# A fused two-layer transformer kernel: the start of the kernel and of its first phase rearranged

## The reference

```python
x = norm(x + L0_attn_ref(x, ...))          # 16 heads of 8, distance bias, head mask; then two norms and a ReLU FFN
x = norm(x + L0_xattn_ref(x, ctx, ctx, ...))   # windowed attention over ctx
x = norm(x + L0_ffn_ref(x, ...))           # 8 experts, top 2
x = norm(x + L1_attn_ref(x, ...))          # rotary, causal
x = norm(x + L1_xattn_ref(x, ctx, ctx, ...))   # gated recurrence
x = norm(x + L1_ffn_ref(x, ...))           # 8 experts, switch (top 1)
```

## Time and profile before

| | us |
|---|---|
| median of 3 runs (1364.31 to 1366.75) | 1365.14 |
| profiled execution | 1372.58 |
| its span, first to last instruction | 1370.8 |
| PE busy | 1208.5 |
| DVE busy | 1042.2 |
| ACT busy | 863.7 |
| POOL busy | 555.5 |

### The profile page before, as it was taken

The page is one execution under the profiler, slowest core; times in us unless marked ns, Lnnn a source line. Parts: engine busy times, 40 slices in busy tenths (PEclk is TensorE's granted clock), DMA queues, the critical chain, the costliest instruction groups (busy, mean ns, idle before and its releaser), DMA issues. The chain is left out here.

```text
span 1370.8 us, 32006 instructions
## 1 busy us (share of the span) xinstructions
PE 1208.5 (88%) x10253; PEld 826.9 (60%) x10253; DVE 1042.2 (76%) x3184; ACT 863.7 (63%) x2474; POOL 555.5 (41%) x831
## 2 busy tenths in 40 slices
PE   3889999999999999988399987999999979998996
PEld 2456666666666666654266654555555556777996
DVE  3477888788888888875678867999999975665465
ACT  2678887878787878764256634666666654453464
POOL 1232334435353534442400027555565312556287
PEclk9999999999999999988599999999999999999999
DMA  6100000001010000000122222013100000000673
GB/s 267 51 17 11 15 17 19 29 17 32 11 32 16 28 17 17 15 13 13 52 74 80 80 70 95 23 37 93 27 24 21 1 3 1 17 17 27 169 209 97
DMA packets 71490, 63.54 MB, mean 46 GB/s; under 512 B 10510, under 2 KB 61586, under 8 KB 70688
## 3 DMA queue, kind: packets, MB, share of 16 engines
q1 hardware_dynamic: 62768, 45.27, 11.3%
q0 software_dynamic: 6400, 12.63, 3.0%
q10 hardware_dynamic: 2160, 3.60, 0.8%
HBM read 43.00 MB, written 18.98 MB: 45 GB/s over the span
## 5 line engine op out<-in xcount | busy, mean ns | idle before, releaser
L767 PE MATMUL e_bank_turned<-c_matrices,e_probs 128*128 128x128 f32 x1024 | 165.9, 286 | 16.3 <-ACT e_probs_t L999 9.0
L693 POOL TENSOR_TENSOR e_rstd<-e_var_eps,c_minus_half 128x1 f32<-128x1 f32 x128 | 71.2, 572 | 253.6 <-DVE e_var_eps L1040 252.9
L999 ACT ACTIVATE e_probs_t<-e_bank_turned 128x512 f32<-128x512 f32 x256 | 155.1, 606 | 16.0 <-PE e_bank_turned L767 14.6
L1127 DVE TENSOR_REDUCE e_neg_max<-e_bank_scores 128x4 f32<-128x512 f32 x160 | 109.6, 685 | 50.8 <-PE e_bank_scores L810 50.4
L767 PEld LDWEIGHTS e_bank_turned<-c_matrices,e_probs 128*128 128x128 f32 x1024 | 116.6, 145 | 40.0 <-issue 16.1
L777 PE MATMUL e_bank_mix<-e_probs_t,e_values 128*32 128x128 f32 x2048 | 113.2, 294 | 15.6 <-ACT e_probs_t L999 14.8
L958 ACT ACTIVATE e_probs<-e_scores,e_neg_max 128x128 f32<-128x128 f32 x384 | 123.3, 410 | 1.1 <-DVE e_neg_max L1163 1.1
L1771 ACT ACTIVATE d_probs_t<-d_bank_turned 128x512 f32<-128x512 f32 x128 | 77.2, 603 | 66.0 <-PE d_bank_turned L1648 66.0
L953 ACT ACTIVATE e_probs<-e_scores 128x512 f32<-128x512 f32 x128 | 82.1, 642 | 42.0 <-DVE e_scores L1160 40.2
L696 POOL TENSOR_TENSOR e_k_by_place<-e_q_k_k,c_matrices 128x512 f32<-128x512 f32 x64 | 66.7, 1042 | 102.8 <-DVE e_q_k_k L1171 102.8
L1753 ACT ACTIVATE d_probs<-d_scores 128x512 f32<-128x512 f32 x128 | 81.0, 632 | 40.6 <-DVE d_scores L1794 38.9
(11 more groups left out here) (330 smaller groups left out, 3289.2 us busy)
## 6 DMA issues: line engine op xcount, KB each, us to landing
streamed<-in_s_up SPq DMA_DIRECT2D x36, 258.0 KB
m_rows<-scratch_sorted SPq DMA_DIRECT2D x72, 64.0 KB
scratch_expert_out<-m_y SPq DMA_DIRECT2D x72, 64.0 KB
sorted_rows<-scratch_sorted SPq DMA_DIRECT2D x40, 65.0 KB, 2.4
e_x_in<-in_x SPq DMA_DIRECT2D x32, 64.0 KB, 1.9
e_ctx_in<-in_ctx SPq DMA_DIRECT2D x32, 64.0 KB, 2.1
up<-in_m_wgv SPq DMA_DIRECT2D x1, 2048.0 KB
up_b<-in_m_bgv SPq DMA_DIRECT2D x1, 2048.0 KB
```

Source lines behind the costliest of these rows:

```text
L767: last = nc.tensor.transpose(turned_bank[:, j * P:(j + 1) * P], pr[k % 3][:, j, :], c["ident"][:])
L999: nc.scalar.activation(pt[k % 2][:], turned_bank[:], ACT.Copy).then_inc(probs_t_ready, 1)
L1127: nc.vector.tensor_reduce(nmax[k % 4][:], bank, AX.X, ALU.max, negate=True).then_inc(max_ready, 1)
```

## The change

Four things are done at once.

- The head mask is loaded as one row into one partition (8 KB), first of all loads. In the encoder PE spreads it over the partitions of the four banks of `quad` with four matmuls against a row of ones. DVE makes `bias0` out of `quad` at tick -5 of the encoder, and PE's `bank_free` waits for that (`bias_made`) for the first units.
- x and ctx of batches 0 to 3 are loaded from the constants phase, x on SP and ctx on ACT, behind the constants. Their buffers and the `x_loaded` semaphores belong to the constants now.
- The `va` tiles are cleared and their columns set by POOL, ahead of its ticks.
- PE no longer waits for `buffers_set`; ACT waits for it ahead of its first copy into `va`.

```diff
@@ load_constants
-    loads.append((c["bias0"][:], d["head_mask"].partition_broadcast(P)))
+    c["head_mask"], c["ones_row"] = sb("head_mask", [1, HEADS, P]), sb("ones_row", [1, P])
+    loads.insert(0, (c["head_mask"][:], d["head_mask"].rearrange("(o h) t -> o h t", o=1)))
+    c["x_in"], c["ctx_in"] = ring(nc, ctx, "c_x_in", [P, P], 4), ring(nc, ctx, "c_ctx_in", [P, P], 4)
+    c["x_loaded"] = [nc.alloc_semaphore(f"x_loaded{k}") for k in range(4)]
...
             for tile, src in loads[0::2]:
                 sp.dma_start(tile, src).then_inc(loaded, 16)
+            for n in range(4):
+                sp.dma_start(c["x_in"][n][:], dram_tile(d["x"], n)).then_inc(c["x_loaded"][n], 16)
...
             for tile, src in loads[1::2]:
                 act.dma_start(tile, src).then_inc(loaded, 16)
+            for n in range(4):
+                act.dma_start(c["ctx_in"][n][:], dram_tile(d["ctx"], n)).then_inc(c["x_loaded"][n], 16)
...
+            nc.vector.memset(c["ones_row"][:], 1.0)
...
-            nc.vector.scalar_tensor_tensor(out=c["bias0"][:], in0=repeat(c["dist"][:], HEADS), scalar=c["nds"][:],
-                                           in1=c["bias0"][:], op0=ALU.mult, op1=ALU.add).then_inc(made, 1)
-            dve.wait_ge(made, 1)
@@ phase_encode, SP
-            for n in range(4):
-                load(n)
@@ phase_encode, POOL, ahead of the ticks
+            for k in range(3):
+                nc.gpsimd.memset(va[0][k][:], 0.0)
+                last = nc.gpsimd.memset(va[1][k][:], 0.0)
+            last.then_inc(buffers_set, 1)
+            pool.wait_ge(buffers_set, 1)
+            for k in range(3):
+                nc.gpsimd.memset(va[0][k][:, :, DH:DH + 1], 1.0)
+                last = nc.gpsimd.memset(va[1][k][:, :, DH:DH + 1], 1.0)
+            last.then_inc(buffers_set, 1)
@@ phase_encode, PE
                 elif k >= 0:
                     pe.wait_ge(probs_ready, k + 1)
+                else:
+                    pe.wait_ge(bias_made, 1)
...
+            for g in range(G):
+                last = nc.tensor.matmul(quad[:, g, :], lhsT=c["ones_row"][:],
+                                        rhs=c["head_mask"][:, G * g:G * g + G, :].rearrange("o h t -> o (h t)"), start=True, stop=True)
+            last.then_inc(mask_spread, 1)
             pe.wait_ge(act_read, 1)
...
-            pe.wait_ge(buffers_set, 2)
@@ phase_encode, ACT
-            act.wait_ge(buffers_set, 2)
...
                     if (n := at(tick, -7)) is not None:
+                        if n == 0:
+                            act.wait_ge(buffers_set, 2)
@@ phase_encode, DVE
-            for k in range(3):
-                nc.vector.memset(va[0][k][:], 0.0)
-                last = nc.vector.memset(va[1][k][:], 0.0)
-            last.then_inc(buffers_set, 1)
...
-            dve.wait_ge(buffers_set, 1)
-            for k in range(3):
-                nc.vector.memset(va[0][k][:, :, DH:DH + 1], 1.0)
-                last = nc.vector.memset(va[1][k][:, :, DH:DH + 1], 1.0)
-            last.then_inc(buffers_set, 1)
-            dve.wait_ge(buffers_set, 2)
...
             for tick in ENCODE_TICKS:
+                if tick == -5:
+                    dve.wait_ge(mask_spread, 1)
+                    nc.vector.scalar_tensor_tensor(
+                        out=c["bias0"][:], in0=repeat(c["dist"][:], HEADS), scalar=c["nds"][:],
+                        in1=quad[:].rearrange("p g (j u) -> p (g j) u", u=P), op0=ALU.mult, op1=ALU.add).then_inc(bias_made, 1)
+                    dve.wait_ge(bias_made, 1)
```

More of the change, by code:

```diff
@@ L176, in load_constants @@
         nds_ready, half_ready = inner.sem("nds_ready"), inner.sem("half_ready")
-        made = inner.sem("constants_made")
         block = inner.enter_context(nc.Block(no_gpsimd_drain=True))
@@ L623, in phase_encode @@
         kept = keep["route0"]
-        xin, cin, xc = tiles("x_in", [P, P], 4), tiles("ctx_in", [P, P], 4), tiles("xT_ctxT", [P, 2 * P], 6)
+        xin, cin, x_loaded, xc = c["x_in"], c["ctx_in"], c["x_loaded"], tiles("xT_ctxT", [P, 2 * P], 6)
         x_bo, x_ln2b, x1_b2, x2_bo = (tiles("x_bo", [P, P], 4), tiles("x_ln2b", [P, P], 5), tiles("x1_b2", [P, P], 3),
@@ L640, in phase_encode @@
         bias3 = ctx.enter_context(nc.sbuf_tensor("e_bias3", [P, 3], F32))
-        x_loaded = [sem(f"x_loaded{k}") for k in range(4)]
         ctx_saved, x3_saved = [sem(f"ctx_saved{k}") for k in range(6)], [sem(f"x3_saved{k}") for k in range(10)]
@@ L652, in phase_encode @@
         var_ready, rstd_ready = [sem(f"var{k}_ready") for k in range(4)], [sem(f"rstd{k}_ready") for k in range(4)]
-        links, buffers_set = sem("links"), sem("buffers_set")
+        links, buffers_set, mask_spread, bias_made = sem("links"), sem("buffers_set"), sem("mask_spread"), sem("bias_made")
         table = table_buffers(nc, ctx, keep["route0"], "t0", table0)
@@ L661, in load @@
             def load(n):
-                if n >= 4:
-                    sp.wait_ge(act_written, ACT_TURNS["x_x1_mix1", n - 6] + 1)
-                    sp.wait_ge(x_summed, n - 3)
+                sp.wait_ge(act_written, ACT_TURNS["x_x1_mix1", n - 6] + 1)
+                sp.wait_ge(x_summed, n - 3)
                 sp.dma_start(xin[n % 4][:], dram_tile(d["x"], n)).then_inc(x_loaded[n % 4], 16)
                 sp.dma_start(cin[n % 4][:], dram_tile(d["ctx"], n)).then_inc(x_loaded[n % 4], 16)
-            for n in range(4):
-                load(n)
             sp.wait_ge(act_written, ACT_TURNS["x_x1_mix1", -2] + 1)
```

## The result

The changed kernel takes 1369.88 us (median of 14 runs, 1366.52 to 1371.7) against 1365.73 for the kernel before (14 runs, 1362.18 to 1367.17): a ratio of 1.0031, 95% interval 1.0024 to 1.0039, so 3.3 to 5.3 us slower. I had forecast 1363.5 and a range up to 1366.6.

A forecast was written before the change was run, and what follows sets the result against it. PE, busy 88% of the span, was taken to bound the kernel, so savings count at its start. Loads -2.1, bias -2.4 and encoder +2.85 make 1.65 us off the median 1365.14: 1363.5, range 1361.3 to 1366.6.

The forecast's parts named there:

- step 1: Constants loads: fewer bytes ahead of the first cast save 2.1 us, so DVE's first cast comes at 10.0.
- step 2: DVE in the constants: the 2.35 us bias leaves, casts stay; PE's encoder starts at 12.06 instead of 16.56.
- step 3: Four mask matmuls ahead of batch 0 on PE: rate turns fast at 16.3, PE through them at 17.95.
- step 5: Bias after `qkk`: 2.35 us, done at 23.45; then bare `distance` 0.86 and scores 1.21, first maximum at 25.57.
- rival (c): Encoder start: TensorE stays at 1.2 GHz up to the first scores, first maximum 29.8, time 1367.7; chance 10%.
- step 6: `va` clears on GpSimd: 0.8 us per large clear, hidden, with cover up to 1.5 us a clear.
- One for one: Whole kernel: later work follows by semaphores and barriers, so the first row maximum's shift moves the end equally.
- Frame 0: Stretch from batch 0's first row maximum to batch 1's: 14.13 us before, against 13.11 for the next frames.
- rival (a): PE stays fast: clock fall misses the first frame (+1.0), masks turn fast sooner (+0.5); gain 3.2, time 1361.9; chance 22%.

The follow-up runs named there:

- e13: Changed kernel with x and ctx loaded at the encoder's start and clears on DVE again; ratio 1.0032 to the kernel before.
- e3: Kernel before with only x and ctx loaded early, clears on GpSimd and PE's wait for them gone; ratio 0.9987 to the kernel before.
- e1: Changed kernel with the four mask matmuls contracting over 128 partitions instead of one; ratio 1.0017 to the kernel before.
- e2: Changed kernel with DVE's bias instruction moved from behind q_k_k to right behind the two bo sums; ratio 1.0005 to the kernel before.
- e4: e2 with the mask row cast to bf16 by ACT under the loads, each mask matmul one pass; ratio 0.9965 to the kernel before.
- the second profile: The unaltered changed kernel, timed and profiled again beside the follow-up runs; first maximum 31.49 us, ratio 1.0022 to the kernel before.
- e8: e2, with its f32 masks, plus 30 bf16 matmuls on ones on PE under the loads; ratio 0.9988 to the kernel before.
- e12: e3 plus 50 bf16 matmuls on ones on PE under the loads of the constants; ratio 0.9976 to the kernel before.

## Why the prediction was wrong

- **Loads (step 1)**: right. First cast 9.94 for 10.0. The saving was 2.17 us for my 2.1. The alternation by whole packets that the Trainium skill tells of (DMA: Bandwidth & Descriptors, "Queues, rings and completion order") is neither shown nor refuted by it: the 1.9 that I drew from it was a bound, with all of SP's x ahead. What the tiles cost can be read from e13, which has none of them behind the constants and makes its first cast at 9.67: 0.27 us (0.40 in e3).
- **DVE in the constants (step 2)**: right, PE started at 12.00.
- **Head mask on PE (step 3): the step that failed.** "The turn can fall anywhere in the masks, and I take the middle, 16.3." I treated the turn as something that a full PE brings about, as the 128-partition matmuls of the trace do, and took it over to a matmul of another shape that no row showed. The runs show that it does not come: 27.7 us of them stay slow. The masks cost 7.19, a little over my upper end, and ended 1.8 us later than forecast; the bias matmuls, transposes and projections behind them stayed slow too, another 1.5. In all 3.3 us by `q_k_k`. The Trainium skill (TensorE: Matmul & The Clock Gate, Part 1) says that activity releases the half rate. In these runs a PE without a gap did not get it released with f32 matmuls over 1, 32 or 64 partitions, and did with 128 (e1).
- **Uncovered bias (step 5)**: the term was right (2.34 and PE's wait), but I priced `distance` and the scores at the fast rate. They ran slow, 0.8 and 1.0 more, as the rate fell 0.4 us after the wait that the change adds. Together 1.85 us, where rival (c) had put such a fall at 1.1; with the 3.3 this is the 5.15 at the first maximum.
- **Clears (step 6)**: right. One clear took 0.52, on DVE 0.48; the Trainium skill (GPSIMD Engine Reference, 4.1 Engine selection), by which one-input work is about as fast on both, was nearer than my 0.8. It changed nothing in the sum.
- **Rival (c)** was this outcome: "TensorE at 1.2 GHz up to the first scores", 29.8 and 1367.7; it gave 30.72 and 1369.88. It too was 0.9 short: it put the scores at 1.4, "about what it was before", where their matmuls had run fast, and slow they took 2.24 to the maximum. I gave it 10%, with "before the wait PE is full from 12.06 to 18.4" against it: the very inference that failed. Its two halves are shown apart. The bias and its wait: without them e2 is at 1.0005. The masks: shortened from 7.19 to 1.88 in e4, they move the kernel from there to 0.9965. e1, which only lets the rate turn within the masks, moves the first maximum by 3.1 us, but its 1.0017 is not clear of the changed kernel's.
- **One for one**: "a shift of the first maximum shifts the end one for one". In the ten comparisons with a ratio, the shift of the first maximum and that of the time (ratio times 1366) agree within 1.3 us in nine and within 1.9 in e1. So it holds, to about the size of what I was forecasting.
- **Frame 0**: I took 13.11 as its length at full rate; it is 11.95. So where the slow stretches fall is worth 2 us in frame 0, not the 1 of rival (a). The gain did not last here: the slow stretch came in frame 1, which took 14.80, and frames 0 and 1 together took 26.75, for 27.24 before. I can't attribute the last microsecond between the shift of the first maximum (+3.5, +4.3 in the second profile), that of batch 3 (+3.0, +5.6) and the medians (+3.0 to +4.2); it is within what these stretches move.

## What to carry to other kernels

A matmul over one partition takes the time of its columns in full, as one over 128 does, and in these runs f32 matmuls over 64 partitions or fewer did not bring TensorE from 1.2 to 2.4 GHz, however long they lasted. Before placing such a spread on a critical path, give it few passes (bf16: 1.88 us instead of 7.19) or keep it off. When a piece of work is moved off an idle start into a chain, look for the place in that chain where its engine is idle anyway: the same bias instruction, one place earlier in DVE's order, gave back 2.3 to 3.6 us. While TensorE waits for the first data, matmuls on a constant can bring it to speed: with 30 of them the best version is 0.60% faster than the kernel before, and 0.35% without. The same addition gave 0.17% from e2 to e8 and 0.11% from e3 to e12, each time less than the intervals can tell, so its sign is likely and its size is not shown.

## What the hardware showed that I had not expected

- f32 matmuls over 1, 32 and 64 partitions left TensorE at 1.2 GHz through 27.7 us without a pause; over 128 partitions, same columns, same place, it went to 2.4 GHz about 5 us after the first. Nothing between 64 and 128 was tried, and no bf16 ones for as long. Why the partitions matter, no run shows.
- Single-partition masks did not keep 2.4 GHz either, 1.7 us after PE had had it: 0.59 mean granted clock over 6.1 us of full PE in e8.
- A clear of 128x512 f32 took GpSimd 0.52 us, next to 0.48 on DVE, while its two-input multiply of that size takes 1.04.
